# The first attention's arguments turned by fp32 products with the identity

## The chip, the cores and the metric

The kernel runs on one core of a Trainium2 chip. The metric is the time of one execution on the device, in microseconds (us); of several runs the median is given. Lower is better.

## The reference, cut to what matters

Two layers work on x of 16 x 256 tokens of width 128, all fp32. Each layer normalises x, sends it through an attention and through a mixture of experts, and adds the product of the attention's output with silu of the experts' output to x. The change lies in the first layer's attention and in the turning of the normalised x.

```
xn = layernorm(x)                       # 16 batches, 256 tokens, 128 wide
q, k, v = split(xn @ W_w.T + W_b)       # 16 heads of width 8
attn = q @ k.T / sqrt(128)              # 256 x 256 for each batch and head
attn = where(causal, -inf, attn) + bias # bias[h, i, j] = rpb[j - i + 255, h]
w = softmax(attn)
s = layernorm(xn + (w @ v) @ proj_w.T + proj_b) * ln_g + ln_b
g = silu(top-1 of 8 experts (xn))
x = x + s * g
```

The second layer has another attention of one head per batch, and top-2 of 8 experts beside a shared one.

## The kernel before, in words

The five engines run instruction lists written out by hand: TensorE (PE), VectorE (DVE), ScalarE (ACT), GpSimd (POOL), and SyncE (SP) for most DMAs. They meet through semaphores, and each engine takes its list in order. Names: `p_...` are PSUM banks, the rest lies in SBUF.

**Front.** x comes in 8 groups of 4 tiles (128 tokens each). DVE measures them, POOL takes the inverse standard deviation, ACT writes the normalised `xn` (line 810), PE turns its four tiles (`turn_x`, line 564) into a bank, ACT copies them to `xt` (line 815). PE projects q and k of a batch (`project`, lines 593 and 594), ACT and DVE split them into bf16 parts that SP sends through memory and back as stacks of 72 rows. POOL loads the bias (line 1255) and fills its masked half with -1e30 (`mask_bias`, line 1260), for four heads at a time. DVE negates it (`negate_bias`, line 948), and `scale_w` has put a minus sign into the weights and the offset of q, so the scores come out negative as well.

**First attention.** The work goes by quads: 4 heads of one batch, 4 quads a batch, 64 quads. For each head the upper 128 queries have 256 keys and the lower ones 128:

- `score`, lines 617 and 618: two bf16 products, 256 and 128 columns, into one of three banks `p_s`. PE makes the scores of quad n + 2 while it turns quad n.
- `row_max`, line 959, DVE: one instruction adds the bias, writes the sum to `high` (256 columns) or `low` (128), and leaves its minimum in `top`. All is negative here, so the minimum is the row maximum with its sign turned.
- `subtract_max`, line 1240, POOL: subtracts `top` from three of the four heads, one instruction for `high` and one for `low`. The fourth head gets its subtraction and exponential on ACT (`exponent`, line 852).
- `turn`, lines 630 to 632, PE: three 128x128 transpositions of fp32 into one of two banks `p_t`.
- `numerator`, lines 860 and 862, ACT: reads the bank, for three heads with exp(-...), into `prob`.
- `weigh`, lines 645 and 649, PE: fp32 products with v, one quad later.

`low` and `high` have three buffers each. Around the quads PE's list places what comes once a batch: `project` of the batch after next, `turn_o` (line 670), `turn_on` (676), `project_o` (682), `values` (606). The gate's products (line 572, 128x8) stand behind quads 0, 1 and 2, the count of tokens per expert (`rank`, line 579) in quad 4, and DVE runs the steps of the routing between its row maxima. POOL scatters tokens to their experts' slots, some each quad from the 12th on (line 346). A loop, with `last` = 64:

```
for n in range(last):
    b, g = divmod(n, quads)
    for x in range(QUAD):
        if n + 2 < last:
            score(pe, n + 2, x)
        turn(pe, n, x)
        ...
        if n and x == WEIGHED:
            weigh(pe, n - 1)
```

**After it** come the experts of the first layer, which wait for the last scattered token. Then `middle`: x is updated and normalised in the same 8 groups, ACT writes `xn` (line 190), PE turns it (`turn`, line 130), ACT copies to `xt` (line 195), PE makes the gate's products (`router`, line 136), and the shared expert starts (`up`, line 153). The second attention and the second experts follow, with transpositions of their own (lines 1533 and 1606).

Of the kernel before, what the change touches and what calls it, by code (L numbers as in the profile page):

```python
# [10 lines left out]
ALU = mybir.AluOpType  # L11
# [77 lines left out]
def middle(R, D, f, sem, before_it, m):  # L89
# [36 lines left out]
    def turn(pe, g):  # L126
        wait_if(pe, s["xt_ok"], g - 1)
        pe.wait_ge(s["xn_ok"], GT * (g + 1))
        for k in range(GT):
            mm = pe.transpose(p_x[g % 2][:, k * P:(k + 1) * P], R.xn[:, GT * g + k, 0:P], R.ident[:])  # L130
        mm.then_inc(s["turned"], 1)
# [218 lines left out]
def first_half(nc, R, D, f):  # L350
# [7 lines left out]
    with ExitStack() as ctx:  # L358
# [5 lines left out]
        def ps(name):  # L364
# [82 lines left out]
            "route", "mask_ok", "ranked", "counted", "routed", "owned", "fill_zero",  # L447
            "e_turned", "e_ids_ok", "e_x_ok", "e_up_ok", "e_pre_ok", "e_hid_ok", "e_down_ok", "e_y_ok", "fill_ok", "biased", "bias_ok",
            "zeros_ok", "ones_ok", "qk_mm", "part1", "part2", "part3", "rest_ok", "v_mm", "v_ok", "scored", "max_ok",
# [109 lines left out]
        def turn_x(pe, g):  # L559
            wait_if(pe, s["xt_ok"], g - 1)  # L560
            for k in range(GT):
                t = GT * g + k
                pe.wait_ge(s["xn_ok"], t + 1)
                mm = pe.transpose(p_s[g % 2][:, k * P:(k + 1) * P], R.xn[:, t, 0:P], R.ident[:])
            mm.then_inc(s["x_turned"], 1)
# [54 lines left out]
        def turn(pe, m, x):  # L620
# [8 lines left out]
            r, bank = m % args, p_t[n % 2]  # L629
            pe.transpose(bank[:, 0:P], low[r][:, x, :], R.ident[:])  # L630
            pe.transpose(bank[:, P:S], high[r][:, x, 0:P], R.ident[:])  # L631
            pe.transpose(bank[:, S:S + P], high[r][:, x, P:S], R.ident[:]).then_inc(s["turned"], 1)  # L632

# [310 lines left out]

        def negate_bias(dve, q):
            dve.wait_ge(s["biased"], q + 1)
            of = bias_q[:, QUAD * q:QUAD * (q + 1), :]
            dve.tensor_scalar(of, of, -1.0, None, ALU.mult).then_inc(s["bias_ok"], 1)

        def row_max(dve, m, x):  # L950
# [4 lines left out]
            if x == 0 and m < quads:  # L955
                dve.wait_ge(s["bias_ok"], m + 1)
            dve.wait_ge(s["scored"], n + 1)
            for t, cols, at, out in ((1, slice(0, S), slice(0, S), high[r]), (0, slice(S, S + P), slice(P, S), low[r])):
                dve.tensor_tensor_reduce(out=out[:, x, :], in0=p_s[n % banks][:, cols], in1=bias_q[:, h, at],  # L959
                                         scale=1.0, scalar=3.0e38, op0=ALU.add, op1=ALU.min,  # L960
                                         accum_out=top[r][:, t, x:x + 1]).then_inc(s["max_ok"], 1)
# [51 lines left out]
        def scale_w(dve):  # L1013
            dve.wait_ge(s["w_in"], 16 * 3)
            dve.tensor_scalar(R.w_qkv[:, 0:P], R.w_qkv[:, 0:P], -SCALE0, None, ALU.mult).then_inc(s["w_ok"], 1)
            dve.tensor_scalar(R.b_qk[:, 0:1], R.b_qk[:, 0:1], -SCALE0, None, ALU.mult).then_inc(s["w_ok"], 1)

# [154 lines left out]
        def _(dve):  # L1172
# [16 lines left out]
            add_bv(dve)  # L1189
            for q in range(quads):  # L1190
                negate_bias(dve, q)
            for m in range(2):
# [110 lines left out]
        def _(pool):  # L1303
# [17 lines left out]
            for g in range(NG):  # L1321
                rstd_x(pool, g)
                if g < quads:
# [8 lines left out]
                      allow_small_or_imprecise_dtypes=True).then_inc(s["tables"], 1)  # L1332
            for q in range(quads):
                mask_bias(pool, q)
            pool.iota(ids_of(R, range(NT)), [[1, NT], [0, 1]], base=0, channel_multiplier=NT)
            for u in range(2):
                pool.memset(fill[u][:], 0.0).then_inc(s["fill_zero"], 1)
            subtract_max(pool, 0)
            subtract_max(pool, 1)
            for n in range(last):  # L1340
                b, g = divmod(n, quads)
# [679 lines left out]
```

## Time and profile before

| | |
|---|---|
| median of 3 runs | 713.06 us (711.78 to 713.98) |
| the profiled execution | 719.64 us |
| its span, first to last instruction | 717.8 us |
| mean granted clock of PE | 0.907 |
| PE busy | 619.3 us, 86% of the span |
| DVE, ACT, POOL busy | 452.1, 378.8, 460.5 us |
| line 630, of 630 to 632, the turning in the quads | 256 instructions, 0.29 us mean |

A group of the profile has a line, an engine, an operation, the tiles written and read, a count, busy time, mean duration and the idle time of the engine before it. The durations of PE overlap, since a product starts before the one ahead has drained: what one costs in a dense row is the distance of the starts. The granted clock is given as a share of 2.4 GHz.

### The profile page before, as it was taken

To read this page: it belongs to the slowest core of one execution; us is meant where nothing else is said; L and a number is where in the kernel's file an instruction comes from. 1 tells how busy PE (TensorE), PEld (TensorE's weight loads), DVE (VectorE), ACT (ScalarE), POOL (GpSimd) and SP (SyncE) were. 2 spreads that over 40 slices of the span, in tenths; PEclk is the share of its full clock that TensorE was granted. 3 is DMA by queue.
4 is the path that set the end of the run, shared out by engine and by line. 5 is a ranking of instruction groups with operands and counts; after the bars stand their busy time and mean duration, and the time that the engine had idled before them with its cause. 6 is when DMAs were issued, how large, how long until landed. Compare 5 with 4: busy or idle time off the path is not lost.

```text
span 717.8 us, 15341 instructions
## 1 busy us (share of the span) xinstructions
PE 619.3 (86%) x4794; PEld 519.3 (72%) x4794; DVE 452.1 (63%) x1824; ACT 378.8 (53%) x905; POOL 460.5 (64%) x526
## 2 busy tenths in 40 slices
PE   4798899999999999899997189998995999999720
PEld 3486577777777777589997178787994999999620
DVE  6627998888888898454443555647771333333796
ACT  6524588887878887644443373323554333333331
POOL 8524377879888889545556563575774566666444
PEclk9557899999999999999999558999998999999955
DMA  8515355544555457247775300421112577772434
GB/s 258 154 66 162 114 183 154 157 140 163 153 157 168 143 165 239 77 141 237 231 235 168 108 15 0 165 92 38 59 54 87 172 238 233 245 238 95 140 118 117
DMA packets 68736, 105.43 MB, mean 147 GB/s; under 512 B 9584, under 2 KB 45936, under 8 KB 68656
## 3 DMA queue, kind: packets, MB, share of 16 engines
q1 hardware_dynamic: 58016, 77.84, 36.2%
q0 software_dynamic: 7616, 17.32, 6.9%
q10 hardware_dynamic: 3024, 9.29, 3.3%
q8 instruction: 40, 0.66, 0.4%
q14 instruction: 40, 0.33, 0.2%
HBM read 69.43 MB, written 34.98 MB: 145 GB/s over the span
## 4 chain that ended last, share of the span: by engine, by line
PE 64%; DVE 13%; POOL 9%; DMA 5%; issue 5%; ACT 3%; SPq 0%; DVEq 0%; ACTq 0%; POOLq 0%
PE a_p_s L1546 7%; PE a_p_s L707 4%; PE a_p_s L617 3%; PE a_p_o L645 3%; PE a_p_s L1571 3%; PE a_p_t L722 3%; POOL slots L1449 3%; PE a_p_t L630 3%; PE a_p_o L722 3%; PE a_p_misc L1558 3%; DMA a_stacks<-parts 2%; PE a_p_t L631 2%; PE a_p_t L632 2%; PE a_p_t L1546 2%; PE a_p_qk L1558 2%
## 5 line engine op out<-in xcount | busy, mean ns | idle before, releaser
L1456 POOL DMA_INDIRECT tok<-a_e_ws,a_stacks x70 | 67.0, 957 | 44.0 <-DVE a_e_ws L1767 33.1
L1240 POOL TENSOR_TENSOR a_high<-a_high,a_top 128x768 f32<-128x768 f32 x42 | 61.6, 1468 | 37.2 <-DVE a_top L959 36.9
L959 DVE CUSTOM_DVE_ANT_0 a_high<-a_p_s,f_shared 128x256 f32<-128x256 f32 x168 | 70.1, 417 | 24.1 <-PE a_p_s L618 22.1
L1449 POOL DMA_INDIRECT slots<-k_xn,k_pos x64 | 63.7, 996 | 30.1 <-issue 15.4
L862 ACT ACTIVATE a_prob_more<-a_p_t 128x384 f32<-128x384 f32 x128 | 63.0, 495 | 37.7 <-PE a_p_t L632 35.9
L1760 DVE TENSOR_TENSOR a_e_ws<-a_p_s,a_e_ws 128x512 f32<-128x512 f32 x39 | 27.0, 692 | 80.8 <-ACT a_e_ws L1673 80.8
L617 PE MATMUL a_p_s<-a_stacks 72*128 72x256 bf16 x256 | 73.4, 288 | 3.4 <-DMA a_stacks<-parts 2.0
L1282 POOL DMA_INDIRECT tok<-a_fill,a_e_ids x46 | 44.3, 963 | 42.8 <-DVE a_fill L1168 35.3
L1546 PE MATMUL a_p_s<-a_fill,a_stacks 128*128 128x256 f32 x236 | 59.1, 388 | 0.0
L618 PE MATMUL a_p_s<-a_stacks 72*128 72x128 bf16 x256 | 57.9, 226 | 0.0
L630 PE MATMUL a_p_t<-k_ident,a_low 128*128 128x128 f32 x168 | 49.2, 293 | 0.4 <-ACT f_w_sh L862 0.3
L1240 POOL TENSOR_TENSOR f_cos_sin<-f_cos_sin,a_top 128x768 f32<-128x768 f32 x22 | 32.6, 1480 | 26.2 <-DVE a_top L959 26.0
L959 DVE CUSTOM_DVE_ANT_0 a_low<-a_p_s,f_shared 128x128 f32<-128x128 f32 x168 | 47.9, 285 | 0.0
L631 PE MATMUL a_p_t<-k_ident,a_high 128*128 128x128 f32 x168 | 47.4, 282 | 0.0
L632 PE MATMUL a_p_t<-k_ident,a_high 128*128 128x128 f32 x168 | 47.4, 282 | 0.0
L797 ACT ACTIVATE f_shared<-f_shared 128x512 f32<-128x512 f32 x46 | 28.9, 630 | 33.9 <-DVE f_shared L1157 33.7
L1546 PEld LDWEIGHTS a_p_s<-a_fill,a_stacks 128*128 128x128 f32 x236 | 42.9, 195 | 4.5
L959 DVE CUSTOM_DVE_ANT_0 f_cos_sin<-a_p_s,f_shared 128x256 f32<-128x256 f32 x88 | 36.9, 420 | 14.0 <-PE a_p_s L618 13.3
L862 ACT ACTIVATE f_w_sh<-a_p_t 128x384 f32<-128x384 f32 x64 | 31.3, 491 | 27.1 <-PE a_p_t L632 25.0
L617 PEld LDWEIGHTS a_p_s<-a_stacks 72*128 72x128 bf16 x256 | 26.3, 103 | 24.0 <-DVE a_top L959 13.8
L959 DVE DVE_READ_ACCUMULATOR2_ANT a_top<- 128x1 f32 x512 | 42.1, 82 | 0.0
L645 PE MATMUL a_p_o<-a_prob_more,a_va 128*32 128x256 f32 x384 | 41.3, 399 | 0.0
(293 smaller groups left out, 1900.1 us busy)
## 6 DMA issues: line engine op xcount, KB each, us to landing
a_stacks<-parts SPq DMA_DIRECT2D x64, 288.0 KB
a_stacks<-in_W SPq DMA_DIRECT2D x39, 384.0 KB, 3.5
a_e_ws<-in_W SPq DMA_DIRECT2D x23, 514.0 KB, 3.4
slots<-a_fill ACTq DMA_DIRECT2D x21, 432.0 KB, 2.8
parts<-a_part SPq DMA_DIRECT2D x32, 192.0 KB, 2.5
a_stacks<-slots SPq DMA_DIRECT2D x35, 144.0 KB, 3.2
a_fill<-slots SPq DMA_DIRECT2D x27, 144.0 KB, 2.4
k_x<-in_x SPq DMA_DIRECT2D x8, 256.0 KB, 4.3
```

Of the source, the lines that this page charges most:

```text
L617: pe.matmul(p_s[n % banks][:, 0:S], q[:, P:S], k, start=True, stop=True)
L618: pe.matmul(p_s[n % banks][:, S:S + P], q[:, 0:P], k[:, 0:P], start=True, stop=True).then_inc(s["scored"], 1)
L630: pe.transpose(bank[:, 0:P], low[r][:, x, :], R.ident[:])
L631: pe.transpose(bank[:, P:S], high[r][:, x, 0:P], R.ident[:])
L632: pe.transpose(bank[:, S:S + P], high[r][:, x, P:S], R.ident[:]).then_inc(s["turned"], 1)
L645: return pe.matmul(p_o[32 * x:32 * (x + 1), S * i2:S * (i2 + 1)], va[b % 2][:, 0, i1, i2, x, :], prob[m % 2][x][:, 0:S], start=start, stop ...
L862: act.activation(prob[m % 2][x], p_t[n % 2][:, 0:S + P], ACT.Exp, scale=-1.0).then_inc(s["prob_ok"], 1)
L959: dve.tensor_tensor_reduce(out=out[:, x, :], in0=p_s[n % banks][:, cols], in1=bias_q[:, h, at], scale=1.0, scalar=3.0e38, op0=ALU.add, op1 ...
L1240: pool.tensor_tensor(arg[:, 0:subtracted, :], arg[:, 0:subtracted, :], top[r][:, t, 0:subtracted].unsqueeze(2).to_broadcast([P, subtracted ...
L1449: pool.indirect_dma_start(D["slots1"], bass.IndirectOffsetOnAxis(ap=R.pos[n][:, t:t + 1], axis=0), R.xn[:, t, :], None).then_inc(done, 16)
L1456: pool.indirect_dma_start(D["tok1"], bass.IndirectOffsetOnAxis(ap=x_in[r][:, k, P:P + 1].bitcast(I32), axis=0), y_out[r][:, k, :], None).t ...
L1546: mm = pe.matmul(ph[u][c // 2][:, c % 2 * SLOTS:(c % 2 + 1) * SLOTS], w[r][:, c * P:(c + 1) * P], x_t[u], start=True, stop=True)
```

## The change

In three places a transposition becomes an ordinary fp32 product of the data, as stationary operand, with the identity: the three blocks of each head in the first attention, the normalised x in front, and the normalised x in the middle. The signs move: q's weights and offset keep their sign, the negation of the bias is gone, and the row maximum's instruction multiplies the sum by -1 instead. So `high`, `low` and `top` hold what they held before. POOL masks the bias of quads 2 and 3 only after the subtractions of quads 0 and 1. `turn_o`, `turn_on`, the experts' and the second attention's transpositions stay.

```diff
@@ middle, turn @@
-            mm = pe.transpose(p_x[g % 2][:, k * P:(k + 1) * P], R.xn[:, GT * g + k, 0:P], R.ident[:])
+            mm = pe.matmul(p_x[g % 2][:, k * P:(k + 1) * P], R.xn[:, GT * g + k, 0:P], R.ident[:], start=True, stop=True)
@@ turn_x @@
-                mm = pe.transpose(p_s[g % 2][:, k * P:(k + 1) * P], R.xn[:, t, 0:P], R.ident[:])
+                mm = pe.matmul(p_s[g % 2][:, k * P:(k + 1) * P], R.xn[:, t, 0:P], R.ident[:], start=True, stop=True)
@@ turn of the first attention @@
-            pe.transpose(bank[:, 0:P], low[r][:, x, :], R.ident[:])
-            pe.transpose(bank[:, P:S], high[r][:, x, 0:P], R.ident[:])
-            pe.transpose(bank[:, S:S + P], high[r][:, x, P:S], R.ident[:]).then_inc(s["turned"], 1)
+            pe.matmul(bank[:, 0:P], low[r][:, x, :], R.ident[:], start=True, stop=True)
+            pe.matmul(bank[:, P:S], high[r][:, x, 0:P], R.ident[:], start=True, stop=True)
+            pe.matmul(bank[:, S:S + P], high[r][:, x, P:S], R.ident[:], start=True, stop=True).then_inc(s["turned"], 1)
@@ row_max @@
-        def negate_bias(dve, q):
-            dve.wait_ge(s["biased"], q + 1)
-            of = bias_q[:, QUAD * q:QUAD * (q + 1), :]
-            dve.tensor_scalar(of, of, -1.0, None, ALU.mult).then_inc(s["bias_ok"], 1)
...
-                dve.wait_ge(s["bias_ok"], m + 1)
+                dve.wait_ge(s["biased"], m + 1)
...
-                                         scale=1.0, scalar=3.0e38, op0=ALU.add, op1=ALU.min,
+                                         scale=-1.0, scalar=3.0e38, op0=ALU.add, op1=ALU.min,
@@ scale_w @@
-            dve.tensor_scalar(R.w_qkv[:, 0:P], R.w_qkv[:, 0:P], -SCALE0, None, ALU.mult).then_inc(s["w_ok"], 1)
-            dve.tensor_scalar(R.b_qk[:, 0:1], R.b_qk[:, 0:1], -SCALE0, None, ALU.mult).then_inc(s["w_ok"], 1)
+            dve.tensor_scalar(R.w_qkv[:, 0:P], R.w_qkv[:, 0:P], SCALE0, None, ALU.mult).then_inc(s["w_ok"], 1)
+            dve.tensor_scalar(R.b_qk[:, 0:1], R.b_qk[:, 0:1], SCALE0, None, ALU.mult).then_inc(s["w_ok"], 1)
@@ the list of POOL @@
-            for q in range(quads):
-                mask_bias(pool, q)
+            mask_bias(pool, 0)
+            mask_bias(pool, 1)
...
             subtract_max(pool, 0)
+            mask_bias(pool, 2)
             subtract_max(pool, 1)
+            mask_bias(pool, 3)
```

POOL's list moves in one place, between the tables of the front and the subtraction of quad 2. Line 1260 (1253 after) is the mask, 1240 (1233 after) the subtraction. Before:

```order
L1260 AFFINE_SELECT f_shared<-f_shared 128x4x128 x4
L1335 IOTA k_xn 128x32
L1337 MEMSET a_fill 128x864 x2
L1240 TENSOR_TENSOR f_cos_sin<-f_cos_sin,a_top 128x768
L1240 TENSOR_TENSOR f_decay<-f_decay,a_top 128x384
L1240 TENSOR_TENSOR a_high<-a_high,a_top 128x768
L1240 TENSOR_TENSOR a_low<-a_low,a_top 128x384
```

and with the change:

```order
L1253 AFFINE_SELECT f_shared<-f_shared 128x4x128 x2
L1328 IOTA k_xn 128x32
L1330 MEMSET a_fill 128x864 x2
L1233 TENSOR_TENSOR f_cos_sin<-f_cos_sin,a_top 128x768
L1233 TENSOR_TENSOR f_decay<-f_decay,a_top 128x384
L1253 AFFINE_SELECT f_shared<-f_shared 128x4x128
L1233 TENSOR_TENSOR a_high<-a_high,a_top 128x768
L1233 TENSOR_TENSOR a_low<-a_low,a_top 128x384
L1253 AFFINE_SELECT f_shared<-f_shared 128x4x128
```

Two of four masks stand ahead of the first subtraction, and one behind each of the first two pairs.

DVE's list, at the step from the front to the first row maxima (line 959, 954 after; each is a record for the sum and one for the minimum). Before:

```order
L942 TENSOR_TENSOR a_part<-a_p_qk,a_part 128x512
L1024 TENSOR_TENSOR k_b_proj<-a_p_t,k_b_proj 128x128
L948 TENSOR_SCALAR f_shared<-f_shared 128x1024 x4
L959 ISA f_cos_sin,a_top<-a_p_s,f_shared 128x256
L959 ISA a_top 128x1
```

and with the change:

```order
L942 TENSOR_TENSOR a_part<-a_p_qk,a_part 128x512
L1019 TENSOR_TENSOR k_b_proj<-a_p_t,k_b_proj 128x128
L954 ISA f_cos_sin,a_top<-a_p_s,f_shared 128x256
L954 ISA a_top 128x1
```

The four negations are gone and nothing takes their place. PE's list has the same operations in the same order.

## Rows read from the trace of the kernel before

**Rows 1.** The page: busy time; granted clock of PE in 40 slices.

```profile
PE 619.3 (86%) x4794; PEld 519.3 (72%) x4794; DVE 452.1 (63%) x1824; ACT 378.8 (53%) x905; POOL 460.5 (64%) x526
PEclk9557899999999999999999558999998999999955
```

**Rows 2.** Busy time by stretches; first numbers are bounds and length in us.

```profile
core 0: us, PE busy (x) PEld busy (x) DVE busy (x) ACT busy (x) POOL busy (x), PEclk, DMA share, GB/s
34.00:58.00 24.00, 24.00 (x140) 20.89 (x138) 9.13 (x59) 7.86 (x19) 8.67 (x10) 0.50 0.20 63
58.00:60.00 2.00, 2.00 (x20) 1.51 (x13) 0.58 (x1) 0.24 (x1) 1.85 (x3) 0.78 0.81 288
96.00:290.00 194.00, 190.03 (x2082) 142.66 (x2074) 169.69 (x995) 157.23 (x396) 166.54 (x179) 1.00 0.52 164
428.00:438.00 10.00, 10.00 (x42) 9.27 (x41) 3.36 (x8) 2.60 (x7) 0.00 (x0) 0.51 0.01 2
438.00:452.00 14.00, 13.13 (x78) 11.25 (x77) 9.27 (x17) 7.53 (x17) 6.94 (x5) 1.00 0.00 1
```

**Rows 3.** Waits of PE's loads, 96 to 290 us: total us, times, longest.

```profile
PEld a_p_s L617 <- DVE a_top L959: 10.7, 26, 0.4
PEld a_p_misc L676 <- DVE a_o_n L969: 4.1, 13, 0.6
```

**Rows 4.** Timeline, POOL: start us, us, engine, line, operation.

```profile
132.03 1.28 POOL L1268 TENSOR_TENSOR k_s<-k_xn,k_b_proj 128x512 f32<-128x512 f32 x1
283.66 1.27 POOL L1268 TENSOR_TENSOR k_s<-k_xn,k_b_proj 128x512 f32<-128x512 f32 x1
```

**Rows 5.** Groups of PE: xcount, busy us, mean ns, idle before.

```profile
L630 PE MATMUL a_p_t<-k_ident,a_low 128*128 128x128 f32 x168 | 49.2, 293 | 0.4 <-ACT f_w_sh L862 0.3
L630 PE MATMUL a_p_t<-k_ident,f_decay 128*128 128x128 f32 x88 | 25.6, 291 | 0.0
L682 PE MATMUL a_p_misc<-k_w_proj,a_o_t 128*128 128x128 f32 x64 | 10.0, 280 | 0.0
```

**Rows 6.** Timeline, PE: from transposition to product to score.

```profile
192.73 0.27 PE L632 MATMUL a_p_t<-k_ident,a_high 128*128 128x128 f32 x1
192.84 0.61 PE L682 MATMUL a_p_misc<-k_w_proj,a_o_t 128*128 128x128 f32 x4
193.29 0.27 PE L617 MATMUL a_p_s<-a_stacks 72*128 72x256 bf16 x1
```

**Rows 7.** Timeline, PE: the third head of a quad.

```profile
181.80 0.22 PE L618 MATMUL a_p_s<-a_stacks 72*128 72x128 bf16 x1
182.02 0.30 PE L630 MATMUL a_p_t<-k_ident,a_low 128*128 128x128 f32 x1
```

**Rows 8.** Timeline, PE: the two long waits, in brackets.

```profile
67.72 0.28 PE L579 MATMUL a_p_misc<-a_mask_bf,k_upper_bf 128*128 128x256 bf16 x1 [3.07 <-DVE a_mask_bf L1055]
81.65 0.44 PE L676 MATMUL a_p_misc<-k_ident,a_o_n 128*128 128x128 f32 x2 [3.35 <-DVE a_o_n L969]
```

**Rows 9.** Timeline, PE: two transpositions at the low clock.

```profile
34.10 0.42 PE L630 MATMUL a_p_t<-k_ident,f_decay 128*128 128x128 f32 x1
34.32 0.42 PE L631 MATMUL a_p_t<-k_ident,f_cos_sin 128*128 128x128 f32 x1
```

**Rows 10.** Timeline, DVE and PE: negations, first scores, first row maximum.

```profile
26.60 2.49 DVE L948 TENSOR_SCALAR f_shared<-f_shared 128x1024 f32<-128x1024 f32 x4
27.79 0.31 PE L618 MATMUL a_p_s<-a_stacks 72*128 72x128 bf16 x1
29.01 0.42 DVE L959 CUSTOM_DVE_ANT_0 f_cos_sin<-a_p_s,f_shared 128x256 f32<-128x256 f32 x1
```

**Rows 11.** Timeline, PE: turning a group of the normalised x.

```profile
9.21 1.63 PE L564 MATMUL a_p_s<-k_ident,k_xn 128*128 128x128 f32 x4 [0.49 <-ACT k_xn L810]
```

**Rows 12.** Timeline, PE: the last two groups of the middle.

```profile
427.61 1.09 PE L130 MATMUL a_p_misc<-k_ident,k_xn 128*128 128x128 f32 x4 [0.40 <-ACT k_xn L190]
430.06 1.09 PE L130 MATMUL a_p_qk<-k_ident,k_xn 128*128 128x128 f32 x4
```

More of the change, by code:

```diff
@@ L447, in first_half @@
             "route", "mask_ok", "ranked", "counted", "routed", "owned", "fill_zero",
-            "e_turned", "e_ids_ok", "e_x_ok", "e_up_ok", "e_pre_ok", "e_hid_ok", "e_down_ok", "e_y_ok", "fill_ok", "biased", "bias_ok",
+            "e_turned", "e_ids_ok", "e_x_ok", "e_up_ok", "e_pre_ok", "e_hid_ok", "e_down_ok", "e_y_ok", "fill_ok", "biased",
             "zeros_ok", "ones_ok", "qk_mm", "part1", "part2", "part3", "rest_ok", "v_mm", "v_ok", "scored", "max_ok",
@@ L1189, in _ @@
             add_bv(dve)
-            for q in range(quads):
-                negate_bias(dve, q)
             for m in range(2):
@@ L1332, in _ @@
                       allow_small_or_imprecise_dtypes=True).then_inc(s["tables"], 1)
-            for q in range(quads):
-                mask_bias(pool, q)
+            mask_bias(pool, 0)
+            mask_bias(pool, 1)
             pool.iota(ids_of(R, range(NT)), [[1, NT], [0, 1]], base=0, channel_multiplier=NT)
```

## The prediction

> **What bounds the kernel now.** I read the page first: TensorE (PE) is busy 86% of the span, more than any other engine, and the clock line shows values about the low level near the front, in the middle and at the end, and full speed between [rows 1]. Then the table by stretches, because the share of busy time is an average. From 96 to 290 us, the bulk of the first attention, PE is marked busy 190.0 of 194 us at a granted clock of 1.00 (2.4 GHz), VectorE (DVE) 169.7 and GpSimd (POOL) 166.5 [rows 2]. The waits of that stretch agree: before a score PE waited for DVE 26 times, at most 0.4 us [rows 3]. One addition on POOL (line 1268) comes once in two batches, that is once in 8 quads, and its first and last place in that stretch are 5 such steps apart: 151.63 us for 40 quads, or **3.79 us a quad** [rows 4]. That is the beat which PE sets. What a longer instruction on PE does here, it does to the end of the kernel, since the experts of the first layer start only after the last quad.
>
> **Price of one product.** The program does 768 transpositions at lines 630 to 632 (64 quads, 4 heads, 3 blocks), all 128x128 fp32. In the groups each of them is one MATMUL record: line 630 has 168 and 88, so 256. A fp32 product is two records: line 682 has 32 products and shows x64 [rows 5]. The timeline has the time of each: the transposition of line 632 begins at 192.73 and its follower 0.11 us later; the two products of line 682 begin at 192.84 and the next score at 193.29, so 0.45 us for four records, 0.222 us a product [rows 6]. The mean durations of 280 to 293 ns are no price, because the records overlap. So a product costs **0.111 us more** than a transposition at full clock. 768 x 0.111 = **85.2 us**, or 12 x 0.111 = 1.33 us a quad.
>
> The Trainium skill (TensorE: Matmul & The Clock Gate, Terms) says that trn2's transpose mode is four times faster for fp32. The trace shows a factor of two at 128 columns; by the page's factor a product would cost 0.44 us, and the surcharge would be three times mine.
>
> **What of this lies beside other work.** A quad of 3.79 us is not pure streaming. (a) At the third head of a quad the first transposition starts 0.22 us after the short score, not 0.06 as at heads without a wait: it wants the PSUM bank that ScalarE (ACT) is still reading for the head two before [rows 7]. With products two heads last 1.66 us and not 1.0, the bank is free in time, and about 0.16 us a quad goes, 51 quads in the stretch: 8 us. (b) Once a batch PE waits for the normalised output (13 times, 4.1 us) [rows 3]; DVE has room then, and I take 3 of it. Together **-11 us**. The bounds are 0 (each wait comes back in another place) and -20, since 190 of 194 are marked busy but the start-to-start times of scores, weighings and bank changes leave some 0.4 us a quad that is no streaming. After it a quad costs 3.79 + 1.33 - 0.22 = 4.90 us of PE. DVE's share of work is 169.7 / 51 = 3.3 us a quad and POOL's 3.3 [rows 2], so both stay below.
>
> (c) Two waits are DVE's own: PE is idle 3.07 us before line 579 and 3.35 us before line 676, where DVE works through the steps of the routing [rows 8]. A slower PE arrives later at both: 13 triples before the first (1.4 us), 11 heads before the second (3.7 us, of which I take 2.6, as DVE waits for scores there too). **-4 us**; bounds 0 and -6.4.
>
> **The clock.** From 34 to 58 us PE is busy 24.00 of 24 us, yet the clock is 0.50, 1.2 GHz [rows 2]: there two transpositions start 0.21 us apart [rows 9]. What runs there are transpositions, bf16 scores, few weighings and the 128x8 products of the gate. In the stretch 58 to 60 it is 0.78, so it rose at about 58.9. Later, at 434.2, the shared expert's dense products begin; the stretch to 438 has 0.51, the next 1.00 [rows 2], so the rise at about 437.8 came behind some 3.6 us of products. The first three quads hold 36 transpositions. If the clock rises as soon as they are products, the 24.8 us from 34.1 to 58.9 become 12.4, plus the 4.0 that the sum has already: -12.4. If it never rises, each of the 36 costs 0.21 rather than 0.11 more: +3.7. I take that it rises after about one quad and may dip in the gate's products: **-8 us**.
>
> The Trainium skill (TensorE: Matmul & The Clock Gate, Part 4: PE-mode transpose) says that transposes do not count as PE-busy and do not bring up the clock. By that rule, the trace agrees for the stretch to 58 us, but cannot show it alone, since the gate's tiny products stand in it too. If the rule is wrong, the -8 becomes +3.7.
>
> **The small edits.** The four negations of the bias (DVE, 2.49 us from 26.60) go; the sign sits in the scale of the row maximum, which I cost at nothing, same instruction and shape. The first row maximum begins at 29.01 though its scores are done at 28.1 [rows 10]: **-0.9 us** (bounds -2.5 and 0). Two of four masks on POOL move behind the first two subtractions, 0.6 us each. POOL is idle before those, and quads 2 and 3 need their bias only after; if that cover were gone, 1.2 us. The 32 transpositions of the normalised x become products: at low clock 0.43 us each against 0.39 at which ACT delivers (4 in 1.63 us) [rows 11], so the last of a group ends later: **+0.7** (0 to +1.6). In the middle, the last two groups are a chain of PE alone, transpositions from 427.61, gate, transpositions from 430.06, gate [rows 12]; 8 products at 1.2 GHz add 8 x 0.213 = 1.7 us, and the two groups before add up to 1.7 more. If products bring the clock up by 431, half of the 6.8 us to 437.8 comes back. **+1.5** (-3 to +3.4).
>
> **Sum.** 85.2 - 11 - 4 - 8 - 0.9 + 0.7 + 1.5 = **+63.5 us**. The profiled execution took 719.64 us (span 717.8, and 1.8 around it), so 783.1. The median of the runs is 713.06, 6.6 below the profiled one, which gives 776.5; I say **776 us**.
>
> **Rivals.**
> 1. *The waits give more* (0.10): PE's slack in a quad is real and most of what it waits for today runs beside the products. For it: the waits of rows 3 and 7. Against: PE is marked busy for 98% of the stretch. All lower bounds together: 85.2 - 20 - 6.4 - 12.4 - 2.5 + 0 - 3 = +41, 754 us; with the clock as I take it, +45.
> 2. *The clock does not help* (0.12): transpositions were never what kept it low, but the gate and the gaps. Then 63.5 + 8 + 3.7 + 1.5 = +77, 790 us; with no wait absorbed at all, up to +92, 805 us.
> 3. *Faster than before* (0.03): a product with the identity costs PE nothing over a transposition, because it is issued as one record or its second pass hides, and what remains is the clock: -12.4 - 0.9 - 3 = -16, 697 us. It would take place in the quads, and decides where the surcharge is under about 16 / 768 = 0.02 us a product; the rows say 0.11 for every fp32 product there is. That the change does not alter the instructions at all belongs here: the list of instructions shows the same names, and only the doubled count in the trace would tell.
> 4. *Four times* (0.02): a product takes four transposition times, 3 x 0.109 x 768 = 251 us more, less the hidden part and the small edits (-22 us): +229, 942 us. This is the factor of the Trainium skill (TensorE: Matmul & The Clock Gate, Terms). Line 682 speaks against it.
>
> The forecast holds 0.73. **Range.** Single terms at their ends are likelier than all at once; from +45 to +82 us I leave out no more than 2 in 10: 758 to 795. A measurement of this kernel tells 0.3% (2 us) from no change. Faster: rival 3, 0.03. Same: 0.01. Slower: 0.96.
>
> **What would show it.** Lines 630 to 632 would have x336 and x176 records, start to start 0.11 each. The addition on POOL would step by about 39 us for 8 quads (now 30.3), the first attention end near 298 + 62 = 360 us, with PE at 1.00 from about 85 on, and PE's waits for DVE gone. The low clock would end near 40 rather than 58.9. DVE's, ACT's and POOL's shares would fall to about 0.7 in the attention. From the first experts on all must be as before but for the middle. I would be wrong if the records per transposition stay one, if a quad steps by over 5.1 us (nothing absorbed) or under 4.7, or if another engine's wait sits before PE in each quad.

## The result and the profile after

| | before | after |
|---|---|---|
| median | 713.52 us of 4 runs (711.78 to 720.55) | 782.18 us of 4 runs (779.85 to 787.32) |
| ratio to before, 95% interval | | **1.0948** (1.0902 to 1.0994) |
| the profiled execution | 719.64 us | 779.85 us |
| its span | 717.8 us | 778.1 us |
| mean granted clock | 0.907 | 0.947 |
| one quad in the even part of the attention | 3.79 us | 5.06 us |

The kernel became 9.5% slower; 776 was forecast, with 758 to 795 as range. The medians lie 69 us apart, the two profiled executions 60. In the later comparisons the kernel before ran 62 times more, with a median of 715.8 us; against that the medians lie 66 us apart. Its profiled execution, 719.64 us at a mean clock of 0.907, is longer and has a lower clock than most of these. The ratios here and below leave out executions over 1.5% above the fastest of their kernel, the medians leave out none. Of the changed kernel's four runs the profiled one is the fastest and has the highest clock; the others have 0.943, 0.939 and 0.937, and 781.2, 783.2 and 787.3 us. So a comparison of the two profiles sets a fortunate execution against an unfortunate one.

The page of the changed kernel, busy time and the clock in 40 slices, against [rows 1]:

```profile
PE 692.7 (89%) x5626; PEld 618.2 (79%) x5626; DVE 457.6 (59%) x1820; ACT 382.3 (49%) x905; POOL 461.8 (59%) x526
PEclk9999999999999999999999965699999899999965
```

PE has 832 records more, which is 768 + 32 + 32: one for every transposition that became a product. In this execution the clock never falls between the front and the end of the attention. Two stretches of the changed kernel (bounds, length, busy time of PE, of its weight loads PEld, of DVE, ACT and POOL, then the clock):

```profile
22.00:60.00 38.00, 33.60 (x306) 29.45 (x307) 24.01 (x122) 18.29 (x45) 18.39 (x21) 1.00 0.48 147
96.00:350.00 254.00, 254.00 (x2645) 221.73 (x2647) 174.57 (x983) 157.03 (x389) 166.35 (x177) 1.00 0.39 121
```

PE is marked busy for 254.00 of 254 us. DVE and POOL do the same work as in [rows 2], but in 254 us. Their waits, where PE's own waits for DVE [rows 3] have gone:

```profile
POOL a_high L1233 <- DVE a_top L954: 50.9, 33, 3.1
DVE a_high L954 <- PE a_p_s L618: 45.8, 67, 1.2
```

The addition that marks 8 quads, line 1261 now, against [rows 4]; five steps again:

```profile
95.06 1.28 POOL L1261 TENSOR_TENSOR k_s<-k_xn,k_b_proj 128x512 f32<-128x512 f32 x1
297.31 1.28 POOL L1261 TENSOR_TENSOR k_s<-k_xn,k_b_proj 128x512 f32<-128x512 f32 x1
```

202.25 us for 40 quads are 5.056 us a quad, 1.265 more than before. Up to quad 16, which follows the front and the low clock of the first quads, nothing is lost in this execution. POOL's first subtraction for it, before and after:

```profile
114.84 1.46 POOL L1240 TENSOR_TENSOR a_high<-a_high,a_top 128x768 f32<-128x768 f32 x1 [0.75 <-DVE a_top L959]
113.08 1.46 POOL L1233 TENSOR_TENSOR a_high<-a_high,a_top 128x768 f32<-128x768 f32 x1 [1.72 <-DVE a_top L954]
```

The groups of line 630 hold twice the records of [rows 5]:

```profile
L630 PE MATMUL a_p_t<-k_ident,a_low 128*128 128x128 f32 x336 | 73.7, 301 | 0.0
L630 PE MATMUL a_p_t<-k_ident,f_decay 128*128 128x128 f32 x176 | 38.5, 301 | 0.3 <-POOL f_decay L1233 0.3
```

And the timeline of one head shows what they cost, against [rows 6, 7]:

```profile
182.11 0.27 PE L617 MATMUL a_p_s<-a_stacks 72*128 72x256 bf16 x1
182.22 0.22 PE L618 MATMUL a_p_s<-a_stacks 72*128 72x128 bf16 x1
182.28 0.44 PE L630 MATMUL a_p_t<-k_ident,a_low 128*128 128x128 f32 x2
182.55 0.39 PE L631 MATMUL a_p_t<-k_ident,a_high 128*128 128x128 f32 x2
182.78 0.39 PE L632 MATMUL a_p_t<-k_ident,a_high 128*128 128x128 f32 x2
183.00 0.60 PE L593 MATMUL a_p_qk<-k_xt,k_w_qkv 128*128 128x256 f32 x2
```

Lines 631 and 632 take 0.22 us each, as forecast, but line 630 takes 0.27. The head has 0.72 us of products, where the three transpositions of a head had 0.334 (0.116, 0.109, 0.109): 0.389 more and not 0.333. The first product starts 0.055 us after the short score at every head; the wait of [rows 7] is gone. The weight loads of the same head, on PEld:

```profile
182.11 0.10 PEld L618 LDWEIGHTS a_p_s<-a_stacks 72*128 72x128 bf16 x1
182.23 0.30 PEld L630 LDWEIGHTS a_p_t<-k_ident,a_low 128*128 128x128 f32 x2
182.44 0.30 PEld L631 LDWEIGHTS a_p_t<-k_ident,a_high 128*128 128x128 f32 x2
```

Two loads take 0.21 to 0.22 us, start to start, and the first of line 630 starts together with the short score.

The two long waits for DVE's routing, against 3.07 and 3.35 us in [rows 8]:

```profile
58.32 0.28 PE L579 MATMUL a_p_misc<-a_mask_bf,k_upper_bf 128*128 128x256 bf16 x1 [1.32 <-DVE a_mask_bf L1050]
...
71.81 0.44 PE L676 MATMUL a_p_misc<-k_ident,a_o_n 128*128 128x128 f32 x2 [1.11 <-DVE a_o_n L964]
```

The first row maximum, without the negations ahead, against 29.01 in [rows 10]:

```profile
27.42 0.42 DVE L954 CUSTOM_DVE_ANT_0 f_cos_sin<-a_p_s,f_shared 128x256 f32<-128x256 f32 x1 [0.64 <-PE a_p_s L618]
```

The end of the attention. Before, PE waited for the first tile of the experts, which waits for the last scattered token:

```profile
298.57 0.61 PE L645 MATMUL a_p_o<-a_prob_more,a_va 128*32 128x256 f32 x8
301.66 0.44 PE L693 MATMUL a_p_qk<-k_ident,a_fill 128*128 128x128 f32 x2 [2.47 <-DMA a_fill<-slots]
```

After, the tile is there when PE arrives:

```profile
358.93 0.61 PE L645 MATMUL a_p_o<-a_prob_more,a_va 128*32 128x256 f32 x8
359.47 0.44 PE L693 MATMUL a_p_qk<-k_ident,a_fill 128*128 128x128 f32 x2
```

So 2.5 us come back there. Last the middle of the changed kernel, the last group, against [rows 12]:

```profile
490.23 2.06 PE L130 MATMUL a_p_qk<-k_ident,k_xn 128*128 128x128 f32 x8
492.08 3.42 PE L136 MATMUL a_p_t<-k_gate_w,k_xt 128*128 128x8 f32 x16
495.35 2.05 PE L153 MATMUL a_p_s<-k_xt,f_w_sh 128*128 128x256 f32 x4
```

### The profile page after: what moved, and what is told of

Same layout as the page of the kernel before. It is cut to its first block, busy times and chain, and to the rows that moved or that the text cites. A ratio compares the mean times of both kernels' runs of the same rounds, so it can differ in the third digit from the quotient of the medians.

```text
span 778.1 us, 17000 instructions
## 1 busy us (share of the span) xinstructions
PE 692.7 (89%) x5626; PEld 618.2 (79%) x5626; DVE 457.6 (59%) x1820; ACT 382.3 (49%) x905; POOL 461.8 (59%) x526
## 4 chain that ended last, share of the span: by engine, by line
PE 75%; POOL 9%; DVE 8%; issue 5%; DMA 2%; ACT 1%; ACTq 0%; DVEq 0%; POOLq 0%; SPq 0%
PE a_p_t L630 9%; PE a_p_t L631 7%; PE a_p_t L632 7%; PE a_p_s L1541 7%; POOL slots L1444 6%; PE a_p_s L617 4%; PE a_p_o L645 4%; PE a_p_s L707 4%; PE a_p_t L722 3%; PE a_p_o L722 3%; PE a_p_misc L1553 2%; PE a_p_o L649 2%; PE a_p_t L1541 2%; PE a_p_qk L1553 2%; PE a_p_s L618 2%
## 5 line engine op out<-in xcount | busy, mean ns | idle before, releaser
L630 PE MATMUL a_p_t<-k_ident,a_low 128*128 128x128 f32 x336 | 73.7, 301 | 0.0
L617 PE MATMUL a_p_s<-a_stacks 72*128 72x256 bf16 x256 | 70.4, 276 | 1.7 <-DVE a_top L954 1.1
L631 PE MATMUL a_p_t<-k_ident,a_high 128*128 128x128 f32 x336 | 65.0, 275 | 0.0
L632 PE MATMUL a_p_t<-k_ident,a_high 128*128 128x128 f32 x336 | 65.0, 275 | 0.0
L1541 PE MATMUL a_p_s<-a_fill,a_stacks 128*128 128x256 f32 x236 | 58.9, 387 | 0.0
L618 PE MATMUL a_p_s<-a_stacks 72*128 72x128 bf16 x256 | 55.6, 218 | 0.0
L630 PEld LDWEIGHTS a_p_t<-k_ident,a_low 128*128 128x128 f32 x336 | 50.4, 190 | 2.6 <-issue 0.4
L632 PEld LDWEIGHTS a_p_t<-k_ident,a_high 128*128 128x128 f32 x336 | 51.0, 192 | 0.0
L631 PEld LDWEIGHTS a_p_t<-k_ident,a_high 128*128 128x128 f32 x336 | 51.0, 192 | 0.0
```

The source lines that it names most:

```text
L617: pe.matmul(p_s[n % banks][:, 0:S], q[:, P:S], k, start=True, stop=True)
L618: pe.matmul(p_s[n % banks][:, S:S + P], q[:, 0:P], k[:, 0:P], start=True, stop=True).then_inc(s["scored"], 1)
L630: pe.matmul(bank[:, 0:P], low[r][:, x, :], R.ident[:], start=True, stop=True)
L631: pe.matmul(bank[:, P:S], high[r][:, x, 0:P], R.ident[:], start=True, stop=True)
L632: pe.matmul(bank[:, S:S + P], high[r][:, x, P:S], R.ident[:], start=True, stop=True).then_inc(s["turned"], 1)
L1541: mm = pe.matmul(ph[u][c // 2][:, c % 2 * SLOTS:(c % 2 + 1) * SLOTS], w[r][:, c * P:(c + 1) * P], x_t[u], start=True, stop=True)
```

## The experiments

All are variants of the changed kernel, so "the signs" (signs and masks moved) are in each. In the diffs `-` is the changed kernel. "Start of quad 3" is the start of POOL's first subtraction for it.

**1. Which part costs: the signs alone.**

```diff
-            mm = pe.matmul(p_x[g % 2][:, k * P:(k + 1) * P], R.xn[:, GT * g + k, 0:P], R.ident[:], start=True, stop=True)
+            mm = pe.transpose(p_x[g % 2][:, k * P:(k + 1) * P], R.xn[:, GT * g + k, 0:P], R.ident[:])
...
-                mm = pe.matmul(p_s[g % 2][:, k * P:(k + 1) * P], R.xn[:, t, 0:P], R.ident[:], start=True, stop=True)
+                mm = pe.transpose(p_s[g % 2][:, k * P:(k + 1) * P], R.xn[:, t, 0:P], R.ident[:])
...
-            pe.matmul(bank[:, 0:P], low[r][:, x, :], R.ident[:], start=True, stop=True)
-            pe.matmul(bank[:, P:S], high[r][:, x, 0:P], R.ident[:], start=True, stop=True)
-            pe.matmul(bank[:, S:S + P], high[r][:, x, P:S], R.ident[:], start=True, stop=True).then_inc(s["turned"], 1)
+            pe.transpose(bank[:, 0:P], low[r][:, x, :], R.ident[:])
+            pe.transpose(bank[:, P:S], high[r][:, x, 0:P], R.ident[:])
+            pe.transpose(bank[:, S:S + P], high[r][:, x, P:S], R.ident[:]).then_inc(s["turned"], 1)
```

> The change with all transpositions kept: only the signs and the two masks move. Theory A (the 60 us come from the products alone, and the low clock from 24.7 to 58.9 us from transpositions that do not raise it): the low clock stays until about 59 us, the first row maximum starts about 1 us earlier, and the time is 0.5 to 1.5 us less than before. Theory B (the low clock came from DVE's negations, which held the first scores back): the clock rises at 35 to 40 us and the time falls by about 10 us.

Measured: 712.83 us median of 10, ratio to before 0.9936 (0.9896 to 0.9977); the first row maximum starts 1.6 us earlier than before, quad 8 starts 4.3 us earlier than in the profile before. From 22 to 60 us the clock is 0.57:

```profile
22.00:60.00 38.00, 35.84 (x200) 29.05 (x201) 17.69 (x97) 15.20 (x36) 15.14 (x18) 0.57 0.39 121
```

The theory that the negations kept the clock low falls. By its interval this version is faster than before, by 0.6%, more than the 0.5 to 1.5 us expected; so is the next one. Experiment 8, with the same signs, has 0.9980 (0.9944 to 1.0016), so the gain of the signs is small and its size is open.

**2. Products in front alone.**

The edits of lines 130 and 630 to 632 as in the first, line 564 stays a product:

```diff
-            mm = pe.matmul(p_x[g % 2][:, k * P:(k + 1) * P], R.xn[:, GT * g + k, 0:P], R.ident[:], start=True, stop=True)
+            mm = pe.transpose(p_x[g % 2][:, k * P:(k + 1) * P], R.xn[:, GT * g + k, 0:P], R.ident[:])
...
-            pe.matmul(bank[:, 0:P], low[r][:, x, :], R.ident[:], start=True, stop=True)
+            pe.transpose(bank[:, 0:P], low[r][:, x, :], R.ident[:])
...
```

> As the run with the signs alone, but the 32 transpositions of the normalised x in front are products. Theory A: the front's products can hold the clock only while they run; quads 0 to 2 still have transpositions, so the clock is low from 28 to 59 us for the most part, and the time is within 1 us of the run with the signs alone. Theory B (in the changed kernel the products in front alone had brought the clock up, and nothing after lets it fall): no low clock before the end of the attention, time 12 to 17 us less than before.

Measured: 713.43 us median of 10, ratio 0.9919 (0.9875 to 0.9963), the same as the signs alone within the intervals; clock 0.73 from 22 to 60 us and 0.88 from 60 to 96. The low clock from 29 us on ended at 46 us, with one more dip to 53, and not near 59 as expected. The front's products alone do not carry the clock through the attention.

**3. Products in front and in quads 0 to 2.** Line 130 transposes.

```diff
-            pe.matmul(bank[:, 0:P], low[r][:, x, :], R.ident[:], start=True, stop=True)
...
+            if m < 3:
+                pe.matmul(bank[:, 0:P], low[r][:, x, :], R.ident[:], start=True, stop=True)
...
+            else:
+                pe.transpose(bank[:, 0:P], low[r][:, x, :], R.ident[:])
...
```

> Products in front and in quads 0 to 2 (36 of 768 triples' blocks), transpositions from quad 3 on and in the middle. Theory A: no low clock before 59 us, saving about 12 us of it against before, less nothing for the products (0.22 at full clock as against 0.21 at low); beat of 3.79 us from quad 16 on as before; time 8 to 14 us less than before. Theory B (the clock rises only where every quad has products): as the run with the signs alone, within 2 us of before.

Measured: 716.12 us median of 10, ratio 1.0004 (0.9959 to 1.0049): **the expected 8 to 14 us did not come.** From 22 to 60 us its clock is low for 14 us, where the profile before has 34 and none was expected:

```profile
22.00:60.00 38.00, 34.73 (x275) 29.46 (x275) 20.93 (x106) 17.57 (x43) 16.64 (x20) 0.82 0.42 126
60.00:96.00 36.00, 31.05 (x288) 22.86 (x289) 31.14 (x158) 21.79 (x54) 17.94 (x22) 0.86 0.50 162
```

Quad 5 starts 6.2 us earlier than before (before first, then this run):

```profile
64.61 1.47 POOL L1240 TENSOR_TENSOR a_high<-a_high,a_top 128x768 f32<-128x768 f32 x1 [4.75 <-DVE a_top L959]
58.42 1.47 POOL L1238 TENSOR_TENSOR a_high<-a_high,a_top 128x768 f32<-128x768 f32 x1 [3.95 <-DVE a_top L959]
```

PE's work takes twice as long at the low clock (a transposition 0.21 us and not 0.109), so 20.5 us less of it are worth 10.2. The 36 products cost 36 x 0.111 = 4.0 at full clock, and 6.2 is left: an estimate that fits this one profile. Then the clock fell again, to 0.86 between 60 and 96 us, where PE waits for DVE's routing. The profiled execution had 5.3 us less than the profiled one before, but only 1.4 less than the median before (715.72), and the median of ten none.

How long the clock was low in a whole execution can be worked out for every run, from its mean clock: (1 - clock) x 2 x span. Ten runs of this version have 114 us on average, ten with the signs alone 121, a difference of 7, give or take 8. Half of that does not pay for the products.

**4. Products in the attention alone.**

```diff
-                mm = pe.matmul(p_s[g % 2][:, k * P:(k + 1) * P], R.xn[:, t, 0:P], R.ident[:], start=True, stop=True)
+                mm = pe.transpose(p_s[g % 2][:, k * P:(k + 1) * P], R.xn[:, t, 0:P], R.ident[:])
...
-            mm = pe.matmul(p_x[g % 2][:, k * P:(k + 1) * P], R.xn[:, GT * g + k, 0:P], R.ident[:], start=True, stop=True)
+            mm = pe.transpose(p_x[g % 2][:, k * P:(k + 1) * P], R.xn[:, GT * g + k, 0:P], R.ident[:])
```

> Products in the first attention alone; front and middle turn x by transpositions. Theory A (the whole surcharge is the attention's, 256 heads x 0.389 us = 99.6 us, less the waits and the clock): 0 to 4 us less than the full change, of it 2 to 3 in the middle, where the changed kernel loses 3.0 us between the last normalised tile and the shared expert. Theory B (front and middle products earn their time through the clock): 3 us or more above the full change.

Measured: 781.05 us median of 4, ratio 1.0908 (1.0824 to 1.0992). That is 1.1 us below the changed kernel, within the 0 to 4 expected. The whole loss is the attention's: 5.06 us a quad, the last weighing ends 64.5 us later than before. From the last normalised tile to the shared expert's first product it needs 4.7 us, the changed kernel 7.7.

**5. The dear first product: short score first.** Line 630 took 0.05 us more than its neighbours. Is that the load of the fp32 weights, which the short score does not cover, or the step from one kind of product to the other?

```diff
-            pe.matmul(p_s[n % banks][:, 0:S], q[:, P:S], k, start=True, stop=True)
-            pe.matmul(p_s[n % banks][:, S:S + P], q[:, 0:P], k[:, 0:P], start=True, stop=True).then_inc(s["scored"], 1)
+            pe.matmul(p_s[n % banks][:, S:S + P], q[:, 0:P], k[:, 0:P], start=True, stop=True)
+            pe.matmul(p_s[n % banks][:, 0:S], q[:, P:S], k, start=True, stop=True).then_inc(s["scored"], 1)
```

> The full change, with the two score products of a head swapped: the one of 128 columns first, the one of 256 last, so the first product of a triple follows 0.11 us of PE work and not 0.055. Theory W (the extra 0.05 us between the two records of line 630 is the load of fp32 weights, which the short score does not cover): the two records start 0.11 us apart, a quad takes 5.06 - 4 x 0.053 = 4.85 us, and the time is about 13 us less than the full change (ratio to before about 1.075). Theory K (it is the step from the 72-row bf16 kind of product to the 128-row fp32 kind): 0.16 us stay, time as the full change within 2 us.

Measured: 772.6 us median of 4, ratio 1.0811 (1.0739 to 1.0882), 9.6 us below the changed kernel's median, where 13 were expected. The timeline of one head:

```profile
181.79 0.22 PE L617 MATMUL a_p_s<-a_stacks 72*128 72x128 bf16 x1
181.85 0.27 PE L618 MATMUL a_p_s<-a_stacks 72*128 72x256 bf16 x1
181.96 0.39 PE L630 MATMUL a_p_t<-k_ident,a_low 128*128 128x128 f32 x2
182.18 0.39 PE L631 MATMUL a_p_t<-k_ident,a_high 128*128 128x128 f32 x2
```

and its beat, four steps:

```profile
137.42 1.28 POOL L1261 TENSOR_TENSOR k_s<-k_xn,k_b_proj 128x512 f32<-128x512 f32 x1
292.40 1.27 POOL L1261 TENSOR_TENSOR k_s<-k_xn,k_b_proj 128x512 f32<-128x512 f32 x1
```

Line 630 now takes 0.22 us, and a quad 154.98 / 32 = 4.84 us, as expected (4.85). The step from one kind of product to the other is still there, and the 0.05 us are gone, so it was the load: the long score's 0.11 us cover it. (64 x 0.21 = 13.6 us; in this execution the clock was low for some 17 us in the first quads, 0.78 from 22 to 60 us, and in the changed kernel's not at all.)

**6 and 7. One product of three.** Does a third of the products cost a third?

```diff
-            pe.matmul(bank[:, 0:P], low[r][:, x, :], R.ident[:], start=True, stop=True)
-            pe.matmul(bank[:, P:S], high[r][:, x, 0:P], R.ident[:], start=True, stop=True)
+            pe.transpose(bank[:, 0:P], low[r][:, x, :], R.ident[:])
+            pe.transpose(bank[:, P:S], high[r][:, x, 0:P], R.ident[:])
```

> Only the last of the three blocks of a head (line 632) is a product, the first two are transpositions; front and middle as in the full change. Theory A (a surcharge of 0.112 us a head, 0.45 a quad, of which 0.29 takes the place of the waits at the third head and once a batch): beat 3.79 + 0.45 - 0.29 = 3.95 us a quad, time 5 to 12 us above the run with the signs alone. Theory C (a third of the products costs a third): beat 3.79 + 1.265 / 3 = 4.21, time 20 to 25 us above it.

Measured: 728.21 us median of 4, ratio 1.0170 (1.0104 to 1.0237). Its beat:

```profile
130.56 1.28 POOL L1261 TENSOR_TENSOR k_s<-k_xn,k_b_proj 128x512 f32<-128x512 f32 x1
259.32 1.28 POOL L1261 TENSOR_TENSOR k_s<-k_xn,k_b_proj 128x512 f32<-128x512 f32 x1
```

Four steps: 128.76 / 32 = 4.02 us a quad, so 0.45 us of surcharge gave 0.23, nearer to 3.95 than to 4.21. The time is 15 us above the signs alone, over the 5 to 12 expected (64 x 0.23 = 15; the expectation had taken off 0.29 for waits, and 0.22 went). With the first block of three as the product:

```diff
-            pe.matmul(bank[:, P:S], high[r][:, x, 0:P], R.ident[:], start=True, stop=True)
-            pe.matmul(bank[:, S:S + P], high[r][:, x, P:S], R.ident[:], start=True, stop=True).then_inc(s["turned"], 1)
+            pe.transpose(bank[:, P:S], high[r][:, x, 0:P], R.ident[:])
+            pe.transpose(bank[:, S:S + P], high[r][:, x, P:S], R.ident[:]).then_inc(s["turned"], 1)
```

> Only the first of the three blocks of a head (line 630) is a product. Theory A with W: this one costs 0.112 + 0.053 less the 0.007 that a transposition there has already, 0.158 us a head or 0.63 a quad, less 0.29 of waits: beat 4.13 us a quad, about 12 us above the run with the last block alone. Theory C or K-free (all products cost the same wherever they stand): as the run with the last block alone, within 2 us.

Measured: 737.05 us median of 4, ratio 1.0284 (1.0212 to 1.0355), 8.8 us above the run with the last block, where about 12 were expected. Its beat:

```profile
134.24 1.28 POOL L1261 TENSOR_TENSOR k_s<-k_xn,k_b_proj 128x512 f32<-128x512 f32 x1
267.45 1.27 POOL L1261 TENSOR_TENSOR k_s<-k_xn,k_b_proj 128x512 f32<-128x512 f32 x1
```

133.21 / 32 = 4.16 us, with 4.13 expected. So 0.64 us of surcharge gave 0.37. The waits of a quad give 0.2 to 0.3 us and no more, and they give it to whichever product comes first. The theory of equal thirds falls: line 632 alone costs 15 of the 69 us, and line 630 costs 9 us more than line 632.

**8. Short score first, with transpositions.** All transpositions are kept as in the first; besides that:

```diff
-            pe.matmul(p_s[n % banks][:, 0:S], q[:, P:S], k, start=True, stop=True)
-            pe.matmul(p_s[n % banks][:, S:S + P], q[:, 0:P], k[:, 0:P], start=True, stop=True).then_inc(s["scored"], 1)
+            pe.matmul(p_s[n % banks][:, S:S + P], q[:, 0:P], k[:, 0:P], start=True, stop=True)
+            pe.matmul(p_s[n % banks][:, 0:S], q[:, P:S], k, start=True, stop=True).then_inc(s["scored"], 1)
```

> The signs alone, all transpositions kept, with the short score first. Theory W: a transposition's single load is nearly covered today, line 630 to 631 takes 0.116 us and the next 0.109, so at most 0.007 x 256 = 1.8 us are to be had: time 0 to 2 us less than the signs alone. Theory D (the beat with transpositions hangs on DVE's start, which wants both scores): no gain or up to 2 us more, since DVE's first instruction reads the long score, which now ends last.

Measured: 713.4 us median of 10, ratio 0.9980 (0.9944 to 1.0016), not to be told from the signs alone (712.83). What the order gives with products it does not give with transpositions.

**9. Products in front and in quads 0 to 7.** As the third, with `m < 8` for `m < 3`.

> Products in front and in quads 0 to 7, transpositions from quad 8 on and in the middle. In the full change quad 8 was 9.8 us early against before, since two idle waits for DVE's routing cover the products there. Theory A (that lead is the clock's and stays): quad 8 starts 5 to 10 us earlier than before, no low clock from 45 to 90 us, time 5 to 9 us less than before, 1 to 5 less than the signs alone. Theory F (the lead was one fortunate course of the clock; products cost in quads 3 to 7 what they bring): as the signs alone within 2 us.

Measured: 714.07 us median of 10, ratio 0.9980 (0.9938 to 1.0022). In its profile quad 8 starts 8.0 us earlier than in the profile before, at 75.8 us, the clock is 0.91 from 22 to 60 and 1.00 from 60 to 96 us, and the span is 7.1 us shorter. But experiments 8 and 10, with transpositions in every quad, start quad 8 at 75.0 and 76.5 us in their profiles: the lead is one over an unfortunate execution. The median is only 1.7 us below before and not below the signs alone.

The clock did gain. By the mean clocks of its ten runs it was low for 102 us an execution, experiment 10 of the same comparison for 119, a difference of 17, give or take 9. Half of it, some 8 us, stands against 32 heads x 0.389 = 12.4 us for the products, of which some 4 lie in the two long waits. So the clock about pays for the products and brings nothing more; this sum is an estimate.

**10. Products in the middle alone.**

```diff
-                mm = pe.matmul(p_s[g % 2][:, k * P:(k + 1) * P], R.xn[:, t, 0:P], R.ident[:], start=True, stop=True)
+                mm = pe.transpose(p_s[g % 2][:, k * P:(k + 1) * P], R.xn[:, t, 0:P], R.ident[:])
...
-            pe.matmul(bank[:, 0:P], low[r][:, x, :], R.ident[:], start=True, stop=True)
+            pe.transpose(bank[:, 0:P], low[r][:, x, :], R.ident[:])
...
```

> Only the 32 transpositions of the middle are products, with the signs; front and attention transpose. Theory A (8 to 16 products on PE's own chain at the low clock): from the last normalised tile to the shared expert's first product 4.8 us before become about 7.8, and the time is 1 to 3 us above the signs alone. Theory B (the products raise the clock before the shared expert and it comes back): the low stretch of about 44 us in the middle ends 3 to 7 us earlier against the last normalised tile, and the time is that of the signs alone or less.

Measured: 715.34 us median of 10, ratio 0.9998 (0.9959 to 1.0037), 2.5 us above the signs alone. Its last groups, on PE:

```profile
424.84 2.05 PE L130 MATMUL a_p_qk<-k_ident,k_xn 128*128 128x128 f32 x8
426.69 3.42 PE L136 MATMUL a_p_t<-k_gate_w,k_xt 128*128 128x8 f32 x16
429.96 1.63 PE L153 MATMUL a_p_s<-k_xt,f_w_sh 128*128 128x256 f32 x3
```

The last normalised tile is done at 422.2, so 7.7 us; with the signs alone 4.7. The middle's products cost 3.0 us.

**11. Is it the kind of work, or how busy PE is?** In quads 0 to 2 each triple of transpositions runs twice; the front has products, line 130 transposes.

```diff
+            for again in range(2 if m < 3 else 1):
+                pe.transpose(bank[:, 0:P], low[r][:, x, :], R.ident[:])
+                pe.transpose(bank[:, P:S], high[r][:, x, 0:P], R.ident[:])
+                mm = pe.transpose(bank[:, S:S + P], high[r][:, x, P:S], R.ident[:])
+            mm.then_inc(s["turned"], 1)
```

> Front with products; in quads 0 to 2 each transposition is issued twice to the same place, so PE is as busy there as with products but does no product; from quad 3 on single transpositions. Theory A (transpositions do not bring the clock up, however dense): the clock is low for most of 28 to 60 us, some 25 to 32 us of it, and quad 3 starts about 45 us or later. Theory G (PE need only be busy): as the run with products in quads 0 to 2, low for 14 to 17 us and then high until about 60 us, quad 3 near 44 us.

Measured: 716.29 us median of 10, ratio 0.9994 (0.9960 to 1.0028). Its stretch:

```profile
22.00:60.00 38.00, 36.38 (x245) 31.25 (x246) 16.90 (x94) 15.21 (x36) 15.07 (x18) 0.69 0.35 112
```

Low for 23.9 us, quad 3 at 45.4 us: nearer to the theory of the kind than to the other, if just below its 25 us. The same number for every profile, the low time between 22 and 60 us, is (1 - clock) x 2 x 38 us:

| quads 0 to 2 with | clock, 22 to 60 us | low for about, us |
|---|---|---|
| transpositions (before, 1, 2, 8, 10) | 0.55, 0.57, 0.73, 0.76, 0.73 | 34, 33, 21, 18, 21 |
| one product in three (6, 7) | 0.66, 0.69 | 26, 24 |
| each transposition twice (11) | 0.69 | 24 |
| products (3, 4, 5, 9, the change) | 0.82, 0.82, 0.78, 0.91, 1.00 | 14, 14, 17, 7, 0 |

The first row and the last do not overlap, though just so (18 and 17), and both spread widely from run to run. So the profiles speak for an earlier rise with products. That it is their kind, and not how dense PE's work is, hangs on the one profile with 24 us, and the sums over ten whole executions do not repeat it: low for 110 us with each transposition twice, 114 with products in quads 0 to 2 (experiment 3), 117 with products in front alone (experiment 2), each give or take 3 to 8. Kind or density is not settled.

## Why the prediction was right, point by point

- **What bounds: right.** PE set the beat before and after; DVE, ACT and POOL do the same work and wait for it.
- **Price of one product: the step that was mis-sized.** 0.111 us more was right for lines 631 and 632. For line 630 the row I took it from has a transposition of 0.11 us ahead, and the loop has a score of 0.055 us. Experiment 5 shows the cause: the fp32 load of 128 columns is not covered. From the short score's start to the product's second record are 0.055 + 0.164 = 0.219 us, and the rows of PEld show two loads to it. The Trainium skill (TensorE: Matmul & The Clock Gate, LDWEIGHTS) gives P / 1.2 ns for P columns, from which I estimate 107 ns for 128; the trace agrees, with two loads in 0.219 us. The term is 256 x 0.389 = +99.6 us, not +85.2.
- **What lies beside other work, (a) and (b): right in kind, too small.** Both waits went. 0.22 us a quad was forecast; 1.556 - 1.265 = 0.29 went, 64 x 0.29 = 18.6 us against 11. (The forecast counted the 51 quads of the even part.) With the price above, a quad steps by 5.06 us where 4.90 was forecast. Experiments 6 and 7 show that it is a pool that the first product empties.
- **(c): right in sum.** 3.07 + 3.35 - 1.32 - 1.11 = 4.0 us, as forecast. Its working has a slip: 1.4 us are 13 products and not 13 triples. In the trace before, 5 heads are turned between the rise of the clock at 58.9 us and line 579, which is 5 x 0.333 = 1.7 us, and 1.75 went there; 2.24 went at line 676.
- **The clock: direction right, size between 7 and 14 us and not settled.** I forecast 8. Up to quad 16, when PE has done 14 quads, the profile has 1.8 us less than before, with 14 x 1.556 = 21.8 us of surcharge. 4.1 of waits in the quads, 4.0 of the long ones and 1.6 of the negations leave some 14 us; part of it are the low stretches near 70 and 84 us, which went too. But the profile before is the latest of its kind: experiments 1, 2, 8 and 10, with the signs moved and transpositions in every quad, start quad 16 at 110.7, 113.7, 107.1 and 107.6 us. Against their mean the same sum leaves about 11 us for the changed kernel's profile and about 7 for experiment 4, whose quad 16 starts at 117.2. Over whole executions the changed kernel was low for 91 us on average of four, the kernel before for 123 of 62, so the second rival, a clock that does not help, is out. That products as such raise the clock, as the forecast took it, fits the profiles (the table) but is not parted from density; and where they are few, they cost about what they bring (experiments 3 and 9). The rise at 58.9 us before came while the quads still had transpositions, so these do not forbid it.
- **The small edits: within their bounds.** The first row maximum came 1.6 us earlier (-0.9 forecast), the middle cost 3.0 us (+1.5 forecast, bound 3.4), the front's products no time that experiment 2 can tell (+0.7 forecast). The signs alone gave 0.6%, more than I allowed, and 0.2% in experiment 8; where the rest of it lies was not tried.
- **Missed:** the 2.5 us at the first expert's tile. The attention ends at 359.5 us, where 360 was forecast.
- **Sum of the profiled executions:** 99.6 - 18.6 - 4.0 - 14 - 1.6 - 2.5 + 3.0 = +62 us, measured +60.3 (span). The 14 of the clock is what the other terms leave up to quad 16, so the sum is no test of it. The forecast's 63.5 was near by luck in part: costs 16 us too low (99.6 - 85.2, and 1.5 in the middle) met credits 17 us too small (41 against 23).
- **Rivals.** Faster, and four times the price, are excluded by the records and by 0.22 us a product, twice the 0.109 of a transposition and not four times. That the waits give more was true in part, and the dear line 630 filled the place.

## What to carry to other kernels

A fp32 transposition on TensorE is one record, a fp32 product with the identity two, and where TensorE sets the beat the second is paid in full, times the number of blocks; only the first 0.2 to 0.3 us a quad hid in waits that the beat contains. Read a price from a row with the same neighbours: a 128-column fp32 product behind a shorter instruction costs its weight load, and the order of two scores was worth 10 us. A better clock in one stretch gives back at most half of the low time that it removes, and the work that brings it has to be paid out of that. And before two single profiles are compared, see where each lies among the runs of its kernel.

## What the runs showed of the hardware

- A 128x128 fp32 product starts its second record 0.111 us after the first behind a 0.11 us instruction, and 0.164 us behind a 0.055 us one (experiment 5).
- A transposition in the same place shows 0.116 us to its follower, as against 0.109 elsewhere: a single load is nearly covered, two in a row are not.
- From 96 us to the end of the attention the changed kernel holds 2.4 GHz with products in place of transpositions, and the kernel before holds it too: transpositions among scores and weighings let the clock stay, while in the first three quads they went with 18 to 34 us at 1.2 GHz.
- The course of the clock differs from run to run of one kernel: the kernel before had mean clocks of 0.900 to 0.932 and 710.7 to 724.1 us in 62 runs.
